# Moving the FFN's weight sums to another stage, and regrouping the probability sums of the cross attention

## What is computed

```
x = x + xattn(layernorm(x), ctx)     # 16 heads, latent keys of width 32, 1601 context rows in each of 8 batches
x = x + attn(layernorm(x))           # 32 heads in 8 groups, 16 gathered cache blocks + 64 new tokens = 576 keys
x = x + ffn(layernorm(x))            # SwiGLU, inner width 1792

def _binary_diff_weight(w, base):    # for w1, w3, w2
    d = w - base
    coeff = jnp.mean(jnp.abs(d))
    return base + coeff * jnp.sign(d)
```

## Time and profile before

| | us |
|---|---|
| median of 3 runs (lowest, highest) | 922.05 (921.88, 923.02) |
| the profiled execution's own time | 923.26 |
| its span | 921.5 |
| PE busy | 876.6 (95%) |
| DVE busy | 602.0 (65%) |
| ACT busy | 519.0 (56%) |
| POOL busy | 416.7 (45%) |
| POOL differences of pieces (line 543), 24 of 2.106 each | 50.5 |
| POOL pair sums (line 550), 48 of 2.386 each | 114.1 |

### The profile page before, as it was taken

One profiled execution on the slowest core, in us unless ns is written; L12 is line 12 of the kernel. 1 busy time (PEld: TensorE's weight loads), 2 busy tenths in 40 slices (PEclk: granted clock), 3 DMA queues, 4 the chain that ended last, 5 costly groups with the idle time before them and its releaser, 6 DMA issues.

```text
span 921.5 us, 15479 instructions
## 1 busy us (share of the span) xinstructions
PE 876.6 (95%) x5386; PEld 665.3 (72%) x5386; DVE 602.0 (65%) x988; ACT 519.0 (56%) x1005; POOL 416.7 (45%) x270
## 2 busy tenths in 40 slices
PE   5889999999998889999999999999999999899998
PEld 3564545555453468888888888888888888688886
DVE  3435557756680527858678586785858769768884
ACT  2355666666666446736557374663637647555552
POOL 3077777877888104423324242342323434154430
PEclk9759999999998899999999999999999999999999
DMA  9844657543462541102011020110201102535531
GB/s 346 312 157 146 241 217 269 209 148 105 146 175 106 197 157 34 59 1 70 23 46 46 0 68 23 46 46 0 68 23 46 35 1 85 190 127 188 192 110 46
DMA packets 46659, 103.72 MB, mean 113 GB/s; under 512 B 11410, under 2 KB 16530, under 8 KB 45714
## 3 DMA queue, kind: packets, MB, share of 16 engines
q1 hardware_dynamic: 46050, 102.86, 33.0%
q10 hardware_dynamic: 560, 0.21, 0.1%
HBM read 97.08 MB, written 1.05 MB: 106 GB/s over the span
## 4 chain that ended last, share of the span: by engine, by line
PE 59%; DVE 2%; ACT 1%; DMA 1%; POOL 0%; SPq 0%; issue 0%
PE psum L1313 11%; PE psum L1299 10%; PE psum L1429 8%; PE psum L1367 8%; PE psum L1325 6%; PE psum L1443 4%; PE psum L1352 3%; PE psum L1343 3%; PE psum L1348 3%; PE psum L1334 1%; PE psum L1344 1%; PE psum L1346 1%; DMA ffn_raw<-in_L_ffn_mean_w_dram 1%; POOL ffn_quant L1814 0%; DVE x L1785 0%; SPq L311 0%
## 5 line engine op out<-in xcount | busy, mean ns | idle before, releaser
L1801 POOL TENSOR_TENSOR head_probs<-head_probs,inverse_den 128x576 f32<-128x576 f32 x128 | 147.5, 1153 | 271.5 <-DVE inverse_den L1654 271.5
L945 DVE TENSOR_REDUCE max_part<-psum 128x1 f32<-128x804 f32 x128 | 121.0, 989 | 66.5 <-PE psum L674 66.5
L844 ACT ACTIVATE probs<-psum 128x512 f32<-128x512 f32 (+1 forms) x208 | 107.9, 601 | 55.2 <-PE psum L695 49.3
L550 POOL TENSOR_TENSOR prob_sums<-probs 128x1024 f32<-128x1024 f32 x48 | 114.1, 2386 | 21.0 <-ACT probs L844 12.1
L1536 ACT ACTIVATE head_probs<-psum,neg_max 128x576 f32<-128x576 f32 x128 | 94.8, 741 | 51.1 <-DVE neg_max L1667 50.4
L1667 DVE TENSOR_REDUCE neg_max<-psum 128x1 f32<-128x576 f32 x128 | 96.9, 757 | 23.8 <-PE psum L1313 22.6
L1313 PE MATMUL psum<-k_high,query_t_high 128*128 (+1 forms) x256 | 86.6, 338 | 2.0 <-DVE coeff L1740 2.0
L1647 DVE TENSOR_TENSOR probs_t_low<-psum,probs_t_high 128x512 fp32r<-128x512 f32 x124 | 84.8, 684 | 1.0
L695 PE MATMUL psum<-q_t,c_t 97*128 97x512 f32 (+1 forms) x208 | 74.2, 439 | 7.1 <-ACT probs L844 5.4
L674 PE MATMUL psum<-c_t,q_t 96*128 96x402 f32 x256 | 77.2, 389 | 3.7 <-DVE max_part L945 2.0
L674 PEld LDWEIGHTS psum<-c_t,q_t 96*128 96x128 f32 x256 | 45.8, 199 | 48.0 <-DVE max_part L945 26.2
(11 more groups left out here) (214 smaller groups left out, 1927.8 us busy)
## 6 DMA issues: line engine op xcount, KB each, us to landing
ctx_t_odd<-in_ctx_dram SPq DMA_DIRECT2D x4, 3202.0 KB, 11.7
w_raw<-in_L_ffn_w_dram SPq DMA_DIRECT2D x24, 448.0 KB, 5.1
w_raw<-in_L_ffn_mean_w_dram SPq DMA_DIRECT2D x24, 448.0 KB, 6.9
ffn_raw<-in_L_ffn_w_dram SPq DMA_DIRECT2D x42, 256.0 KB, 3.8
ffn_raw<-in_L_ffn_mean_w_dram SPq DMA_DIRECT2D x42, 256.0 KB, 4.1
cache<-in_ctx_dram SPq DMA_DIRECT2D x3, 3202.0 KB, 10.7
wq_nat<-in_L_attn_wq_dram SPq DMA_DIRECT2D x32, 256.0 KB, 3.0
wo_nat<-in_L_attn_wo_dram SPq DMA_DIRECT2D x32, 256.0 KB, 2.7
```

Of the source, the lines that this page charges most:

```text
L550: pool.tensor_tensor(sums[u][:, :], prob_buffer(b, 2 * u)[:, :], prob_buffer(b, 2 * u + 1)[:, :], ALU.add).then_inc(s_add, 1)
L844: act.activation(prob_buffer(b, t)[0:rows, half * BANK:(half + 1) * BANK], psum[0:rows, n % SCORE_BANKS, :], ACT.Exp, scale=XSCALE).then_i ...
L945: dve.tensor_reduce(max_part[:, qt, pair:pair + 1], psum[:, bank:bank + 2, 0:PIECE_KEYS], AX.XY, ALU.max).then_inc(s_max, 1)
L1801: pool.tensor_tensor(probs[:, qt, :], probs[:, qt, :], rden[:, qt:qt + 1].to_broadcast([P, KEYS]), ALU.mult).then_inc(s["norm"], 1)
```

## The change

1. The pieces of FFN weights leave the cross attention: no `load_pieces`, no `difference`, no `abs_sum` there.
2. They come into the grouped attention, seven pieces of 1024 columns instead of eight of 896, one per group and weight in the groups 0 to 6. Two slots hold them (`w_slot0`, over the first chunk's place, and `w_slot1`). GpSimd subtracts behind its scalings in the heads 1, 2 and 3 (`piece`), ScalarE sums absolutes in the heads 2, 3 and the next group's 0, ahead of its wait for the mix, and GpSimd adds each result to a total (128x1). The product with ones and the `coeff` move into group 7's output, and with them the load of the first chunk, which waits for the slots.
3. GpSimd adds probabilities into three sums of four or five tiles in place of six of two: nine adds of 128 rows and one of 65 per batch. The sums are double (`sums[3 * (b % 2) + k]`).
4. The tail's value products run in one round with the products of the first sum, the products of the other two sums in a second. TensorE's `denominators` waits for the copied parts (`s_cp`) instead of the placed values; its second maximum product now waits for those, and VectorE copies u ahead of placing values.

The diff, cut to its core:

```diff
-PIECE = WSIZE // P // BATCH
+PIECE = WSIZE // P // (NKV - 1)
...
+SUM_OF = {1: 0, 2: 0, 3: 0, 5: 1, 6: 1, 7: 1, 9: 2, 10: 2, 11: 2, 12: 2}
+SUMMED = len(SUM_OF)
...
@@ cross_attention, gpsimd
-            def add_pair(b, u):
-
-                pool.wait_ge(s_exp, HALVES * b + 4 * u + 4)
-                wait(pool, s_den, b)
-                pool.tensor_tensor(sums[u][:, :], prob_buffer(b, 2 * u)[:, :], prob_buffer(b, 2 * u + 1)[:, :],
-                                   ALU.add).then_inc(s_add, 1)
...
+            def add_tile(b, t):
+
+                rows = slice(0, rows_of(t))
+                total = sums[3 * (b % 2) + SUM_OF[t]]
+                first = t - 1 not in SUM_OF
+                pool.wait_ge(s_exp, HALVES * b + 2 * t + 2)
+                if first:
+                    wait(pool, s_den, b - 1)
+                else:
+                    pool.wait_ge(s_add, SUMMED * b + sums_after(t) - 1)
+                pool.tensor_tensor(total[rows, :], (prob_buffer(b, t - 1) if first else total)[rows, :],
+                                   prob_buffer(b, t)[rows, :], ALU.add).then_inc(s_add, 1)
...
-            for s in range(BATCH):
-                for u in range(ADDS):
-                    if u in DIFF_AT:
-                        difference(s, DIFF_AT.index(u))
-                    add_pair(s, u)
...
+            for b in range(BATCH):
+                for t in SUM_OF:
+                    add_tile(b, t)
...
@@ cross_attention, tensor
                 elif i == 1:
                     pe.wait_ge(s_d, 2 * (b - 1))
+                    if b + 1 < BATCH:
+                        pe.wait_ge(s_cnat, b + 2)
...
             def denominators(b):
                 if b + 3 < BATCH:
-                    pe.wait_ge(s_cnat, b + 4)
+                    pe.wait_ge(s_cp, b + 4)
...
-                for k in range(ADDS // 2):
-                    pe.wait_ge(s_add, (ADDS + 1) * b + (2 * k + 2 if k < ADDS // 2 - 1 else ADDS + 1))
...
+                pe.wait_ge(s_exp, HALVES * (b + 1))
+                pe.wait_ge(s_add, SUMMED * b + 3)
+                for half in range(2):
+                    at = 2 * LKV * half
+                    mm = pe.matmul(psum[at:at + LKV, U_BANK, :], c_nat[0:TAIL, b % 3, KT - 1, :],
+                                   prob_buffer(b, KT - 1)[0:TAIL, half * BANK:(half + 1) * BANK], start=False, stop=True)
+                    add_up(half, 1, 0, True, False)
+                mm.then_inc(s_pv, 1)
+                pe.wait_ge(s_add, SUMMED * (b + 1))
+                for half in range(2):
+                    add_up(half, 0, 1, True, True)
+                    mm = add_up(half, 1, 2, False, True)
                 mm.then_inc(s_den, 1)
...
-                values(b, UNITS - 1)
...
@@ attention_and_ffn, sync
             with sp.Fori(1, NKV) as g:
+                sp.wait_ge(s_abs, 3 * (g - 1) + 1)
+                load_piece(g - 1, 0)
+                load_piece(g - 1, 1)
                 for i in range(REP):
 
+                    if i == REP - 1:
+                        sp.wait_ge(s_abs, 3 * (g - 1) + 2)
+                        load_piece(g - 1, 2)
...
@@ attention_and_ffn, tensor
                 if i == 0 and last:
                     for qt in range(TT):
                         output(g, qt)
+                        if qt == 2 and isinstance(g, int):
+                            pe.wait_ge(s_tot, 3 * (NKV - 1))
+                            pe.wait_ge(s["ql"], n + 2)
+                            pe.matmul(psum[:, head_bank(i + 1), 0:3], ones[:, :], total[:, :], start=True,
+                                      stop=True).then_inc(s_all, 1)
+                    if isinstance(g, int):
+                        pe.wait_ge(s_co, 1)
...
-            pe.matmul(psum[:, 7, 0:3], ones[:, :], total[:, :], start=True, stop=True).then_inc(s_all, 1)
-            pe.wait_ge(s_co, 1)
...
@@ attention_and_ffn, scalar
+            def abs_sum(g, i):
+
+                if i == 1 or (isinstance(g, int) and (g == 0 and i == 0 or g == NKV - 1 and i > 0)):
+                    return
+                k = (i - 2) % 3 if i else 2
+                act.wait_ge(s_pdiff, 3 * g + (i - 1 if i else 0))
+                act.activation(slot(k)[:, 0, :], slot(k)[:, 0, :], ACT.Abs,
+                               accum_out=part[:, k:k + 1]).then_inc(s_abs, 1)
...
@@ attention_and_ffn, gpsimd
+                piece(g, i)
...
+            def piece(g, i):
+
+                if i > 0 and not (isinstance(g, int) and g == NKV - 1):
+                    pool.wait_ge(s_piece[i - 1], 32 * (g + 1))
+                    pool.tensor_tensor(slot(i - 1)[:, 0, :], slot(i - 1)[:, 0, :], slot(i - 1)[:, 1, :],
+                                       ALU.subtract).then_inc(s_pdiff, 1)
+                if i == 1 or (isinstance(g, int) and (g == 0 and i == 0 or g == NKV - 1 and i > 0)):
+                    return
+                k = (i - 2) % 3 if i else 2
+                pool.wait_ge(s_abs, 3 * g + (i if i else 1))
+                pool.tensor_tensor(total[:, k:k + 1], total[:, k:k + 1], part[:, k:k + 1], ALU.add).then_inc(s_tot, 1)
```

More of the change, by code:

```diff
@@ L327, with sums_after @@
 C_WIDTH = MAIN + TAIL
-DIFF_AT = (0, 1, 2)
-ABS_AT = 3
+SUM_OF = {1: 0, 2: 0, 3: 0, 5: 1, 6: 1, 7: 1, 9: 2, 10: 2, 11: 2, 12: 2}
+SUMMED = len(SUM_OF)
+def sums_after(t):
+    return sum(1 for i in SUM_OF if i <= t) + (t + 1 in SUM_OF and t not in SUM_OF)
 COMPRESS_BANK = (4, 3, 6) + (4,) * (BATCH - 3)
@@ L452, in pairs_summed @@
         g = KT * b + t - 4
-        return (g // KT) * (ADDS + 1) + (g % KT) // 2 + 1 if g >= 0 else 0
+        return (g // KT) * SUMMED + sums_after(g % KT) if g >= 0 else 0
     def query_copy(j, odd):
@@ L477, in _ @@
         def _(sp):
[L478 to L482, removed]
             def place_keys(b):
@@ L516, in _ @@
             load_context(core, ctx_t, sp, 2, 0)
-            for i in range(3):
-                load_pieces(0, i)
             place_keys(1)
@@ L719, in denominators, with add_up @@
                     pe.wait_ge(s_d, 2 * b)
-                for k in range(ADDS // 2):
-                    pe.wait_ge(s_add, (ADDS + 1) * b + (2 * k + 2 if k < ADDS // 2 - 1 else ADDS + 1))
-                    for half in range(2):
-                        for odd in range(2):
-                            at = 2 * LKV * half + LKV * odd
-                            mm = pe.matmul(psum[at:at + LKV, DEN_BANK, :], ones[:, :],
-                                           sums[2 * k + odd][:, half * BANK:(half + 1) * BANK],
-                                           start=(k == 0), stop=(k == ADDS // 2 - 1))
+                def add_up(half, odd, k, start, stop):
+                    at = 2 * LKV * half + LKV * odd
+                    return pe.matmul(psum[at:at + LKV, DEN_BANK, :], ones[:, :],
+                                     sums[3 * (b % 2) + k][:, half * BANK:(half + 1) * BANK], start=start, stop=stop)
+                pe.wait_ge(s_exp, HALVES * (b + 1))
[10 more added lines that the diff above has]
+                    mm = add_up(half, 1, 2, False, True)
                 mm.then_inc(s_den, 1)
@@ L1218, in attention_and_ffn @@
     total = core.sb("abs_total", [P, 3], ctx=own)
+    part = core.sb("abs_part", [P, 3], ctx=own)
+    slots = [over("w_slot0", [P, 2, PIECE], F32, "ffn_raw0"), core.sb("w_slot1", [P, 2, PIECE], ctx=own)]
+    s_piece = [core.sem(f"w_piece_in{k}", own) for k in range(3)]
+    s_pdiff = core.sem("w_piece_diff_done", own)
+    s_abs = core.sem("w_piece_abs_done", own)
     coeff = core.sb("coeff", [P, 3], ctx=own)
@@ L1237, in attention_and_ffn, with slot @@
     s_out = core.sem("out_written", own)
+    wnames = (("w1", "mean_w1"), ("w3", "mean_w3"), ("w2", "mean_w2"))
+    flat = {n: arg[n].rearrange("r c -> (r c)").rearrange("(p f) -> p f", p=P) for pair in wnames for n in pair}
+    def slot(k):
+        return slots[k % 2]
     def quant_of(c):
@@ L1277, in _ @@
                     load_output_weight(core, qo, sp, g, i)
-            for c in range(1, CH):
-                if c < SLOTS:
+            for c in range(CH):
+                if c == 0:
+                    sp.wait_ge(s_abs, 3 * (NKV - 1) + 1)
+                elif c < SLOTS:
                     sp.wait_ge(s["s"], TT * NH)
```

64 lines of the change are left out of this document (17 added, 47 removed).

## The result

The changed kernel takes **937.08 us** (median of 4 runs, 936.14 to 938.95) against 921.96 us for the kernel before (920.55 to 923.02): ratio 1.0156, 95% interval 1.0126 to 1.0186. Beside the kernel before on another chip the ratio was 1.0176 (1.0137 to 1.0214). The forecast was 935.5 us, slower by 1.5%. The profiled execution took 937.82 us, its span 936.0 us, 14.5 us more than before.

The account below looks back on a forecast made before the run. TensorE, busy 876.6 of 921.5 us, was taken as the bound. Cross attention -8.3, grouped attention's start -0.6, product in group 7 +0.3, GpSimd's differences +22.1 gave +13.5, so 935.5 us; range 929 to 942, widened to 923 to 942.

Parts of the forecast that it names:

- The collision: Grouped attention, heads 1 to 3: GpSimd's difference holds up VectorE's two-SBUF-operand instructions, so TensorE waits; 22.1 us lost.
- hidden: Rival, grouped attention: VectorE keeps its turn or GpSimd comes late, so GpSimd's work costs nothing; 913.5 us, chance 0.16.
- only head 1: Rival, grouped attention: only the head with two output-weight instructions is held, 10.2 us lost; 923.7 us, chance 0.06.
- The clock falls in the grouped attention: Rival: with three waits a group, TensorE runs some stretches at 1.2 GHz; beyond 945 us, chance 0.03.
- GpSimd bound: Rival, cross attention: sums in place cost 10% more, 2.4 us a batch, and eat the gain; 941.5 us, chance 0.04.
- The range of 929 to 942: Whole kernel: the forecast's own range, from bounds of 5 to 10 us won and 16 to 27.6 lost.
- the next head's first maximum starts at 480.30: Grouped attention, end of head 1: VectorE's maximum starts 1.56 us late, not at 478.74, so TensorE waits 1.46 us.
- Cross attention: All batches: fewer denominator rounds, scores moved up and shorter waits, less a cost in the last batch; 8.3 us won.
- The rounds themselves: Cross attention: one 0.90 us denominator round goes in batches 0 to 6; the tail's own round gives 0.37 in 0 to 4.
- In 5 and 6 the scores wait for that copy already, so nothing there: Cross attention, batches 5 and 6: removing the tail's own round wins nothing, as scores already wait for the maximum's row copy.
- Batch 7: Cross attention, last batch: GpSimd sets the pace, its chain of ten sums ends later; 0.7 us lost.
- Start of the grouped attention: TensorE's 1.96 us wait for the coefficients goes, leaving the low part of the queries as last need; 0.6 us won.

Follow-up runs that it names:

- the kernel with pairs: The change, but in the last batch GpSimd adds six pairs and TensorE runs four rounds, tail tile by itself: 929.71 us, ratio 1.0077 to the kernel before.

## Why the prediction was right, and where its terms were off

**The collision** was forecast step by step and came so. Counted from the end of GpSimd's fourth scaling, the difference was to end at 2.80 us, the first line-1667 instruction (1658 before) at 3.34, the second at 3.94, the low part of the mix at 4.55: measured 2.80, 3.34, 3.94 and 4.55. The rows that carried this were two chance meetings and line 987 in the earlier trace rows. The rivals "hidden" and "only head 1" fell with the rows of head (2, 2). "The clock falls in the grouped attention" fell with a granted clock of 1.00 from 337 us to the end, and "GpSimd bound" in its size: TensorE waits for sums in batch 7 alone. The range of 929 to 942 doesn't come out of the bounds named for it, which give 928 to 944, and its 16 us has no working.

**Its size**, 22.1 us, was 19.6: 1.34, 0.74 and 0.72 us a group for 1.46, 0.85 and 0.85. The mechanism held; the step that was mis-sized is "the next head's first maximum starts at 480.30". I left 0.72 us between the starts of the mix part and of the maximum, the distance in the kernel before, where VectorE had waited for the mix part:

```profile
478.02 0.69 DVE L1639 TENSOR_TENSOR mixed_t_low<-psum,mixed_t_high 128x512 fp32r<-128x512 f32 x1 [0.55 <-ACT mixed_t_high L1528]
478.74 0.76 DVE L1667 TENSOR_REDUCE neg_max<-psum 128x1 f32<-128x576 f32 x1
```

With work queued, VectorE starts the maximum after 0.60 (480.19 to 480.79), in all 21 collisions; after a wait for the mix part it is 0.71 us or more each time. That is 0.12 us a head, 0.36 a group, the whole gap. That TensorE would wait in one place was wrong as well; it waits in two in head 1, and the idle time that the trace shows (0.92 us there) is less than the head's growth.

**Cross attention:** the forecast had 8.3 us won, measured from batch 0's maxima on are 5.1.
- The rounds themselves were right: 1.15 us a batch for 1.27 in the batches 1 to 4, -0.87 for -0.90 in batch 6, and batch 0 gave 0.5 more.
- "In 5 and 6 the scores wait for that copy already, so nothing there": the price of the round was right and its cover wasn't followed. Taking the tail's round away from in front of the copy of the maxima left TensorE idle for 1.20 us in the batches 5 and 6, and the clock fell. In the profiled execution that cost 1.5 us in batch 5, in others in both. The prediction weighed a fall only in the grouped attention, and dismissed it on one wait of 1.63 us; there TensorE's clock did stay up with 96.7% busy time.
- Batch 7: 0.7 us forecast, 2.27 measured. GpSimd's last sum ended 22.12 us after batch 6's products with `wv_u` began, 20.72 before, so the chain cost 1.4. The ten sums were priced by their duration, 2.387 us, which is the same in place. But a sum that adds to the one just made starts 2.49 us after it (288.40, 290.89, 293.37), where independent pairs started 2.33 apart before (289.45, 291.78, 294.10). The last nine took 22.03 us, 0.5 more than nine durations; that is most of the 0.7 by which this term was too small. Behind a wait of 5.15 us TensorE had the lower clock, and the last round and the copy took 3.35 us instead of 2.48 (295.76 to 299.11; 302.64 to 305.12): 0.87.

**Start of the grouped attention:** -0.6 forecast, +0.91 measured. The products with `wv_u` behind the long wait took 0.80 us more at the lower clock. That doesn't explain it: in the kernel with pairs they took 1.12 us, and the stretch was 48.57 us all the same (48.28 in the change, 47.37 before). The wait for the coefficients went, as forecast (1.96 to 1.41 us, now for line 1635), but its 0.6 us don't show in the stretch. The clock falls once near this place in both profiles, at 344 to 348 before and 334 to 337 now. Over the profiles of the changed kernels the stretch takes 47.6 to 49.7 us, with the same work of TensorE in it, and the longest are those where the clock is low for 7 us near its end instead of 3; what the gain was lost to isn't separated by any run.

So the sum of 13.5 against 14.5 is closer than its terms: the collision 2.6 too large, the cross attention and what the clock did behind it 4.7 too small, and the 0.9 us by which this execution came sooner to batch 0's maxima, which nothing in the change explains. The place, the mechanism and the sign were foreseen; that the sum came within 1 us is luck.

## What to carry to other kernels

Work put on an idle engine isn't free if the two engines share a port: look where the other's two-operand instructions stand, and count turns, not busy time. Here one wait, which holds GpSimd back by 1.2 us, turned a loss of 1.6% into a gain of 0.7%. Before taking out an instruction that seems to cost its own duration, look which wait it stands in front of, and whether another piece of work can be put there.

## What the runs showed of the hardware

- VectorE instructions with two operands in SBUF and GpSimd's take turns, instruction by instruction, while both have one waiting: 2.88 us for a 0.68 us instruction against 1024 columns, 1.78 against 512. VectorE instructions that read PSUM run beside GpSimd with their own durations (0.69 us).
- TensorE's clock fell to its lower level some 2 us behind a wait of 1.20 us in 11 of 14 batches, and behind one of 1.05 us at the end of batch 6 in 9 of 12. It did not behind 0.70 us in the batches 0 to 4, behind 0.56 and 0.38 us repeated in each group, nor behind single waits of 1.41 us (348.1) and 1.63 us. The length of one wait doesn't decide it, and what does isn't shown.
- The time to batch 0's maxima ranged from 56.5 to 61.9 us over the eleven profiles of the changed kernels, with nothing changed there: differences of a few us are to be read from an event behind it.
